# Moving the Wk projection of the next tile behind the second chunk's attention block in stage A of a two-stage kernel (gated linear attention, then a channel mix)

## What is computed

```python
def attn(x):                       # x is layernorm(x)
    q = silu(x @ Wq.T)
    f = sigmoid(x @ Wk.T)
    g = log_sigmoid(f)
    k = 1.0 - f
    v = x @ Wv.T
    # per head and token t: S = exp(g_t)[:, None] * S + k_t[:, None] * v_t[None, :]
    #                       o_t = q_t @ S
    return rmsnorm(o) * norm_w @ Wo.T

def ffn(x):                        # x is layernorm(x); x_prev is x shifted by a token
    xr = mu_r * x + (1 - mu_r) * x_prev
    xk = mu_k * x + (1 - mu_k) * x_prev
    return sigmoid(xr @ W_r.T) * (square(relu(xk @ W_k.T)) @ W_v.T)

x = x + layernorm(attn(layernorm(x)))
x = x + layernorm(ffn(layernorm(x)))
```

## Time and profile before

| what | value |
|---|---|
| timed runs | 5723.63 and 6199.23 us, median 5961.43 us |
| profiled execution, its own time | 5723.81 us |
| its span on the slowest core (core 4) | 5722.1 us |
| spans of the 8 cores | 5704.0 to 5722.1 us |
| mean granted clock of TensorE, 8 cores | 0.802 to 0.805 of full speed |
| granted clock in stage A, core 4 | 0.81 |
| packets of the DMAs | 121.83 MB, 21 GB/s on average |

### The profile page before, as it was taken

How to read it: one execution, slowest core, us unless ns; L and a number is a source line. 1 busy time by engine, 2 the same in 40 slices (tenths; PEclk the granted TensorE clock), 3 DMA queues, 4 the chain that set the end, 5 groups by cost and what they waited for, 6 DMA issues and landing times.

```text
span 5722.1 us, 65819 instructions; the slowest of 8 cores (5704.0 to 5722.1 us)
## 1 busy us (share of the span) xinstructions
PE 3462.7 (61%) x26574; PEld 2613.1 (46%) x26608; DVE 1954.0 (34%) x1944; ACT 987.6 (17%) x1529; POOL 587.8 (10%) x307
## 2 busy tenths in 40 slices
PE   0566666666666666661166656676656776656665
PEld 0344444444444444450154444554444555444554
DVE  1333333333333333332133333233333233343323
ACT  0222222222222222220011101111111111110110
POOL 1111111111111111111200000000000000000000
PEclk9778888888887788885588778887778887777887
DMA  2000000000000000002200000000000000000000
GB/s 82 26 15 15 15 15 15 15 16 16 16 15 16 14 16 16 15 12 66 70 15 15 23 23 23 15 8 23 23 23 23 23 1 23 23 23 23 23 8 8
DMA packets 114735, 121.83 MB, mean 21 GB/s; under 512 B 3683, under 2 KB 107270, under 8 KB 114438
## 3 DMA queue, kind: packets, MB, share of 16 engines
q1 hardware_dynamic: 114438, 117.63, 6.6%
HBM read 83.00 MB, written 34.62 MB: 21 GB/s over the span
## 4 chain that ended last, share of the span: by engine, by line
PE 52%; DVE 28%; ACT 6%; DMA 5%; issue 5%; POOL 2%; DVEq 1%; ACTq 0%; SPq 0%; POOLq 0%
PE p_pj L250 39%; PE p_st L231 4%; DVE b_sb L331 4%; PE p_pj L400 3%; PE p_O L514 1%; DVE r_a L207 1%; PE p_O L531 1%; DMA outT<-x_sb 1%; DVE p_A L457 1%; PE p_A L479 1%; DVE A_l L462 1%; DVE A_h L460 1%; ACT xsq_bf L552 1%; ACT L204 1%; DVE tmp L341 1%
## 5 line engine op out<-in xcount | busy, mean ns | idle before, releaser
L250 PE MATMUL p_pj<-o_pair,woh 128*128 128x256 bf16 x2176 | 426.2, 303 | 545.3 <-POOL o_pair L763 312.7
L250 PEld LDWEIGHTS p_pj<-o_pair,woh 128*128 128x128 bf16 x2176 | 233.3, 108 | 607.1 <-issue 560.5
L231 PE MATMUL p_st<-x_sb,onesc 128*1 128x256 f32 x544 | 181.3, 507 | 472.9 <-ACT oB L897 272.5
L250 PE MATMUL p_pj<-ln_h,wkh 128*128 128x256 bf16 x1088 | 308.7, 284 | 199.6 <-DVE ln_l L613 199.6
L250 PE MATMUL p_pj<-xk_h,wv2h 128*128 128x256 bf16 x1088 | 313.7, 288 | 118.9 <-DVE xk_l L821 118.9
L231 PEld LDWEIGHTS p_st<-x_sb,onesc 128*1 128x1 f32 x544 | 55.1, 104 | 598.2 <-issue 573.7
L250 PE MATMUL p_pj<-o_pair,wol 128*128 128x256 bf16 x1088 | 328.1, 302 | 0.0
L250 PE MATMUL p_pj<-xk_l,wv2h 128*128 128x256 bf16 x1088 | 314.0, 289 | 0.0
L250 PE MATMUL p_pj<-xr_h,wrh 128*128 128x256 bf16 x1088 | 297.6, 274 | 25.5 <-DVE xk_l L938 25.2
L250 PE MATMUL p_pj<-xk_h,wv2l 128*128 128x256 bf16 x1088 | 312.7, 287 | 0.0
L250 PE MATMUL p_pj<-ln_h,wqh 128*128 128x256 bf16 x1088 | 309.0, 284 | 2.5 <-ACT fq_sb L648 2.5
(11 more groups left out here) (176 smaller groups left out, 7866.1 us busy)
## 6 DMA issues: line engine op xcount, KB each, us to landing
x_sb<-xT SPq DMA_DIRECT2D x17, 1024.0 KB, 5.4
o_scr<-o_stage SPq DMA_DIRECT2D x68, 256.0 KB, 2.3
oB<-o_scr SPq DMA_DIRECT2D x17, 1024.0 KB, 5.5
xB<-xT SPq DMA_DIRECT2D x17, 1024.0 KB, 5.4
outT<-x_sb SPq DMA_DIRECT2D x16, 1024.0 KB, 4.7
wstage<-wkT SPq DMA_DIRECT2D x8, 512.0 KB
wstage<-wqT SPq DMA_DIRECT2D x8, 512.0 KB
wstage<-wvT SPq DMA_DIRECT2D x8, 512.0 KB
```

Of the source, the lines that this page charges most:

```text
L231: op("tensor", lambda e, ci=ci: e.matmul(p_st[0:1, 0:TILE], onesc[:], x_ap[:, ci, :], start=(ci == 0), stop=(ci == NCH - 1)), wait=wv if c ...
L250: e.matmul(bank[:, 0:TILE], wop[:, ci, dj * 128:(dj + 1) * 128], xop[:, ci, :], start=first, stop=last),
```

## The change

In the loop of stage A the call of `a_wk(p)` is moved from before `a_gla(2 * q + 1)` to after it, right ahead of `a_wq(p)`. Nothing else is changed.

```diff
--- before.py
+++ after.py
@@ -666,10 +666,10 @@
             a_vproj(2 * q + 1)
         if p < nt:
             a_ln(p)
-            a_wk(p)
         if q >= 0:
             a_gla(2 * q + 1)
         if p < nt:
+            a_wk(p)
             a_wq(p)
             if p + 1 < nt:
                 a_stats(p + 1)
```

## The result

The changed kernel is slower by 0.74%: the ratio of its times to those of the kernel before is 1.0074, with a 95% interval of 1.0056 to 1.0092. The profiled execution took 5764.4 us against 5723.8 before, 40.6 us more; the forecast was 8 us less, 5716 us, and its range ended at 5765 us. The profiled execution is just inside it; the timed runs on which the comparison rests, 5762 to 5780 us, are mostly above. The sign was wrong, and the size small on either side.

A forecast was written before the change was run, and what follows sets the result against it. The prediction took a serial chain across engines as the bound; its terms, -0.85 - 0.6 - 1.6 + 2.55, gave -0.5 us per tile, times 16 -8 us, so 5716 us, range 5675 to 5765 us.

The forecast's parts named there:

- The bound: Whole kernel: a serial chain passing from engine to engine, its length per tile being what counts; PE busy only 61%.
- the slower rival: Wait at Wq paid in full, clock gives nothing back: +1.7 us per tile, 5751 us; chance 0.33.
- term 3: Wk projection behind a_gla runs at a higher clock: -1.6 us per tile, end points 0 and -1.59.
- Term 1: First matmuls of the second chunk's a_gla run during v evacuation and a_ln: -0.85 us per tile, 0 if cover fails.
- Term 2: Rest of the second chunk's a_gla, faster if the clock rises: -0.6 us, the middle between 0 and -1.16.
- Term 4: Wq directly behind Wk: new PE wait of 2.48 us and lower clock, +2.55 us per tile, lower end +0.7.
- The drain: Table switches between Wk and Wq: by the skill's rule some 2.8 us more per tile; the prediction followed the trace instead.
- The small things: One table load fewer and k_sb no longer beside a_gla's DVE work: 0 each; statistics bounded by 0.5 us either way.
- the bound of 0.5 us: Statistics at the tile's end: may begin at another clock phase, at most 0.5 us either way.
- another sum: Upper end of the range: slower rival plus 0.5 us for statistics and Wk at 23.10 us, some 5765 us.

The follow-up runs named there:

- e3: Kernel before with only the first 24 matmuls of the second chunk's a_gla put ahead of a_ln; period 139.7 us, 3.7 us below the kernel before.
- e14: Changed kernel with matmuls that nothing reads in all long PE waits, the one at Wq included; period 138.9 us, ratio 0.9894 to the unfilled kernel before.
- e13: Changed kernel with nine matmuls that nothing reads in PE's wait at Wq only; ratio 1.0039 to the kernel before, period 144.3 us.
- e15: Kernel before with matmuls that nothing reads in PE's long waits, but none at Wq; period 136.8 us, spans 5594 to 5624 us.
- e9: Kernel before with one, three or six row copies on DVE ahead of a_bc, no order changed; periods 144.5, 146.4 and 148.2 us.
- e1: Changed kernel with four PSUM banks instead of two for Wq; period 141.1 us against 146.8, spans 0.9% less than the kernel before.
- e6: Kernel before with three more ACT copies ahead of Wq's first evacuation, making PE wait there; period 150.6 us, 6.9 us more.

## Why the prediction was wrong

The bound was read rightly, and so was the mechanism of the slower rival, which had 0.33; two steps failed: the forecast counted on the clock being up when Wk begins (term 3), and it put unchanged code at nothing. The second is the larger. Point by point:

- Term 1, -0.85 us: right as it stood; DVE's first operation follows a_ln at once (749.30). Its cover held, kt was ready. What it missed is e3: the same matmuls early, with Wk left in front, are worth 3.7.
- Term 2, a_gla at -0.6: it measured -0.3 (15.26 us on average against 15.53 from DVE's first operation to the last square). The clock came up in the second half in few tiles.
- Term 3, Wk at -1.6: this step failed. Wk took 22.3 us in the tile shown and began at 0.50. The prediction chose the v projection as the nearest row, which starts at 1.00 behind a_gla; the other end point, that Wq had started low behind the same a_gla, was the right one. e14, at a clock of 0.95, shows Wk 1.4 us shorter: the price was right, that it would be got was not.
- Term 4, Wq at +2.55: right. The stretch between the two last evacuations is 25.3 us, as in tile 0, the wait 2.5 us in each tile; e13 shows 1.6 us of it as the clock's. The drain that the Trainium skill names on the page ScalarE: Activation LUTs, under "What ACT_TABLE_LOAD costs", does not show in these waits either: each is as long as tile 0's.
- The small things: the statistics at the tile's end kept their 13.3 us. But the bound of 0.5 us was for the statistics alone, and the prediction named no term for the unchanged code behind them, which it so put at nothing without a reason: a_gla(2q) and the second v projection became 0.8 and 0.9 us longer, with the clock. This is the largest gap, 1.7 of the 3.7 us by which the sum was off; term 3 is 1.5 and term 2 is 0.3.

Added up: -0.85 - 0.3 - 0.1 + 2.6 + 1.7 makes +3.1 us, against +3.2 measured. The slower rival, +1.7, had the first four about right and lacked the fifth. The span of the slowest core came out 40 us longer, less than the 47 us of stage A, because core 4 had an unusually long stretch behind stage A before. The range ended at 5765 us by another sum (slower statistics, and Wk like tile 0's); that the profiled execution falls just inside it is luck. For the unchanged pieces the cause is shown: at the same clock they are as long in either order, e14 and e15 bring the v projection to the same 11.3 us, and e3 and e9 make it long without a new wait and without moving Wk. What stays open is why the clock comes up in some tiles and not in others, that is, what a given shift will do.

## What to carry to other kernels

When two blocks change places, ask for each wait of one engine what other engine's work it had covered, and price the wait that opens with the clock behind it: here a wait of 2.5 us cost 5.7 (e1) and one of 3.4 us cost 6.9 (e6). Moving only the few instructions that another engine is waiting for, and leaving the long block as their cover (e3), was worth more than moving the block. In this kernel, where the matmul engine is idle for some 40% of the time, unchanged stretches have a short and a long duration, by the clock that they get, and the profile of before shows which one they have: count how many tiles have the short one before taking it for granted.

## What the runs showed of the hardware

Forty-eight matmuls of 512 columns took 11.3 us where the granted clock was 1.00 throughout and 13.0 to 13.4 us where its mean was 0.83 to 0.87, and nothing in between in 240 tiles. A delay in stage A's chain cost more than itself there: 0.5, 1.4 and 2.8 us of it gave 0.9, 3.0 and 4.5 us per tile, while the stretch behind stage A became 13 to 19 us shorter in all. Matmuls without use gave time back: with all long waits filled, and PE busy for 88% of the stretch, stage A's period fell from 143.6 to 136.8 us in the old order and from 146.8 to 138.9 in the new, with the clock at 0.95 instead of about 0.8. Half filled they gave almost nothing (143.6 to 142.5 in the old order).

One lead was not tried. The eight scans of a chunk take 2.85 us in the first a_prep of a round and 10.70 in the second, for the same operation and size (chain of the kernel before, start us, us, what):

```profile
670.48 2.85 DVE b_sb L331 x8
...
681.62 10.70 DVE b_sb L331 x8
```

The second set runs while POOL works on the first chunk's kt and kx, the first set while POOL is idle; the 7.8 us stand in the chain of each tile in every version here. That the one causes the other is not shown.
